# Cross attention: how the softmax sums are inverted, who multiplies, and where the first residual block is loaded

## The reference, cut to what matters

```
scores = q @ k.T / sqrt(32)          # 154 context rows, with a mask on the first 512 query rows of a batch
out    = softmax(scores) @ v         # = (exp(scores - max) @ v) / sum(exp(scores - max))
x2     = x1 + out @ Wo.T + bo        # projection and residual, done in the next stage
```

## Time and profile before

| | |
|---|---|
| time, median of 3 runs (lowest, highest) | 3250.19 us (3243.59, 3250.36) |
| the profiled execution: its time, its span | 3238.29 us, 3236.2 us |
| cross attention, first PE instruction to the next stage's first | 2386.25 to 2696.28 us |
| busy over the whole span: PE, DVE, ACT, POOL | 2957.8, 2091.0, 1609.1, 1750.3 us |
| busy in the 34 us from 2586 to 2620: PE, DVE, ACT, POOL | 33.55, 31.83, 25.63, 0.00 us |
| inversions L1525 in the whole stage | 64, 111.0 us busy |

### The profile page before, as it was taken

The page is one execution under the profiler, slowest core; times in us unless marked ns, Lnnn a source line. Parts: engine busy times, 40 slices in busy tenths (PEclk is TensorE's granted clock), DMA queues, the critical chain, the costliest instruction groups (busy, mean ns, idle before and its releaser), DMA issues. The chain is left out here.

```text
span 3236.2 us, 42137 instructions
## 1 busy us (share of the span) xinstructions
PE 2957.8 (91%) x15214; PEld 1738.2 (54%) x15214; DVE 2091.0 (65%) x3796; ACT 1609.1 (50%) x2996; POOL 1750.3 (54%) x742
## 2 busy tenths in 40 slices
PE   8999699999999999999999999969959997889388
PEld 5878355455455454554554555338745554777333
DVE  4332777777777777776777777436549894665323
ACT  2222166666667666666676666622227672222111
POOL 1000179788889797888897989830001102332265
PEclk9999599999999999999999999979969998999589
DMA  7444754745655647456456563438765442442621
GB/s 230 173 175 156 183 104 98 160 97 112 147 108 117 141 99 160 98 109 150 102 116 139 108 147 79 102 105 266 202 158 157 135 139 89 152 147 105 214 69 36
DMA packets 186936, 435.77 MB, mean 135 GB/s; under 512 B 30557, under 2 KB 51966, under 8 KB 166716
## 3 DMA queue, kind: packets, MB, share of 16 engines
q1 hardware_dynamic: 161718, 286.39, 30.6%
q0 software_dynamic: 24448, 145.80, 21.4%
q10 hardware_dynamic: 576, 1.05, 0.1%
HBM read 180.67 MB, written 127.18 MB: 95 GB/s over the span
## 5 line engine op out<-in xcount | busy, mean ns | idle before, releaser
L791 DVE TENSOR_REDUCE part_max<-ps_s 128x1 f32<-128x512 f32 x2048 | 1269.6, 682 | 351.8 <-PE ps_s L692 351.6
L891 ACT ACTIVATE probs<-ps_st 128x512 f32<-128x512 f32 x2048 | 1059.9, 602 | 542.5 <-PE ps_st L711 536.7
L641 POOL TENSOR_TENSOR added<-added,probs 128x2048 f32<-128x2048 f32 x256 | 1181.7, 4616 | 105.0 <-ACT probs L891 83.0
L711 PE MATMUL ps_st<-q_stack,k_stack 98*128 98x512 f32 x2048 | 873.8, 430 | 6.6 <-ACT probs L891 5.3
L692 PE MATMUL ps_s<-k_stack,q_stack 96*128 96x512 f32 x2048 | 832.3, 413 | 22.7 <-POOL max_parts L631 20.8
L711 PEld LDWEIGHTS ps_st<-q_stack,k_stack 98*128 98x128 f32 x2048 | 391.7, 192 | 526.0 <-ACT probs L891 357.4
L722 PE MATMUL ps_pv<-probs,v_sb 128*32 128x512 f32 x4096 | 551.6, 611 | 0.0
L692 PEld LDWEIGHTS ps_s<-k_stack,q_stack 96*128 96x128 f32 x2048 | 400.0, 195 | 120.7 <-DVE part_max L791 35.6
L649 POOL DMA_DIRECT2D probs<-probs x128 | 111.3, 874 | 193.3 <-PE ps_pv L722 175.6
L722 PEld LDWEIGHTS ps_pv<-probs,v_sb 128*32 128x32 f32 x4096 | 81.0, 108 | 163.9 <-ACT probs L891 135.7
L641 POOL TENSOR_TENSOR added<-probs 128x2048 f32<-128x2048 f32 x32 | 146.6, 4580 | 23.9 <-ACT probs L891 23.9
(11 more groups left out here) (274 smaller groups left out, 3512.2 us busy)
## 6 DMA issues: line engine op xcount, KB each, us to landing
probs<-probs POOLq DMA_DIRECT2D x128, 1024.0 KB, 7.1
xq_stack<-q_parts SPq DMA_DIRECT2D x64, 384.0 KB, 4.7
q_parts<-k_stack SPq DMA_DIRECT2D x88, 256.0 KB, 4.1
q_stack<-q_hi SPq DMA_DIRECT2D x64, 256.0 KB, 6.6
k_stack<-k_hi SPq DMA_DIRECT2D x64, 256.0 KB, 9.4
x_in<-in_x_rows SPq DMA_DIRECT2D x8, 1024.0 KB, 7.2
q_hi<-qk_h_out SPq DMA_DIRECT2D x8, 1024.0 KB
q_lo<-qk_l_out SPq DMA_DIRECT2D x8, 1024.0 KB, 6.3
```

The source lines that it names most:

```text
L641: pool.tensor_tensor(added[:, w % 2], left, probs[:, k % RING], ALU.add).then_inc(added_up, 1)
L711: pe.matmul(ps_st[:, n % BANKS], k_stack[0:TOP, w // BPB, j, k * P:(k + 1) * P], q_stack[:, w % 4, j], start=True, stop=True).then_inc(ite ...
L791: dve.tensor_reduce(part_max[:, s:s + 1], ps_s[:, (w * SLOTS + s) % BANKS], AX.X, ALU.max)\
L891: act.activation(probs[:, k % RING, j], ps_st[:, n % BANKS], ACT.Exp, scale=SCALE).then_inc(item_used, 1)
```

## The change

Units are now treated in pairs p (units 2p and 2p+1), for the first 15 pairs:

- The two units' sums, one row per head, go by DMA to DRAM (`sums_to_columns`) and come back as a 128x32 tile `dens_c` (`columns_back`). DVE inverts that tile once a pair (`invert(p)`). The inverses go out again (`inverses_out`) and are read back into `attn_out`, each head's row spread on its 32 partitions by one of four DMAs (`inverses_spread`). POOL multiplies `attn_out` with the weighted values, 128x1024 at once, and SP stores the two units.
- The weighted values wait in six buffers instead of two. `sums_out` waits for the DMA of the sums instead of the multiplication.
- The last two units are inverted and multiplied by DVE, each inversion as one instruction of 128x512, after the split of the preloaded block and only when the stores of all 15 pairs have landed.
- POOL's weight splits stand behind the products of pairs 1, 3, 4, 6 and 7.
- The first block of x1 is no longer loaded in cross attention. `shared_feed_forward` loads it, 1 MB, as its very first DMA, ahead of the six small loads.

```diff
-        for u in range(UNITS + 3):
+        def sums_to_columns(p):
+            sp.wait_ge(sums_done, 2 * p + 2)
+            sp.dma_start(dens_rows, sums[0:P:HD]).then_inc(dens_moved, 16)
+        def columns_back(p):
+            sp.wait_ge(dens_moved, 16 * (p + 1))
+            sp.dma_start(dens_c[:], dens_rows.rearrange("j w (c e) -> (j w c) e", e=PER)).then_inc(dens_laid, 16)
+        def inverses_out(p):
+            sp.wait_ge(inverted, p + 1)
+            sp.dma_start(recip_rows.rearrange("j w (c e) -> (j w c) e", e=PER), dens_c[:]).then_inc(recip_moved, 16)
+        def inverses_spread(p):
+            if p:
+                sp.wait_ge(out_stored, 32 * p)
+            sp.wait_ge(recip_moved, 16 * (p + 1))
+            for j in range(HEADS):
+                sp.dma_start(attn_out[j * HD:(j + 1) * HD], recip_rows[j].partition_broadcast(HD)).then_inc(recip_loaded, 16)
...
+        for u in range(UNITS):
+            if u % 2 and u >= 3:
+                sums_to_columns((u - 3) // 2)
+            if u % 2 == 0 and u >= 4:
+                inverses_out((u - 4) // 2)
             if exists(u + 1):
                 rows_into_place(u + 1)
+            if u % 2 and u >= 3:
+                columns_back((u - 3) // 2)
+            if u % 2 == 0 and u >= 4:
+                inverses_spread((u - 4) // 2)
+            if u % 2 and u >= 5:
+                store((u - 5) // 2)
...
-                        sp.dma_start(next_x[:, c], x1_rows.rearrange("(n t p) d -> n t p d", t=TPB, p=P)[0, c])\
-                          .then_inc(next_loaded, 16)
...
+        p = PAIRS - 2
+        inverses_out(p)
+        inverses_spread(p)
+        store(p)
+        store(p + 1)
...
+                for p in range(PAIRS - 1):
+                    pool.wait_ge(recip_loaded, 16 * HEADS * (p + 1))
+                    pool.wait_ge(raw_done, 2 * p + 2)
+                    r = 2 * p % RAWS
+                    pool.tensor_tensor(attn_out[:], attn_out[:], attn_raw[:, r:r + 2], ALU.mult).then_inc(normalized, 1)
+                    if p in SPLIT_AFTER:
+                        split(SPLIT_AFTER.index(p))
...
+                def normalize_last(u):
+                    w = u % 2
                     dve.wait_ge(sums_done, u + 1)
-                    dve.reciprocal(sums[:, u % 2, cols], sums[:, u % 2, cols]).then_inc(inverted, 1)
+                    dve.reciprocal(sums[:, w], sums[:, w]).then_inc(last_inverted, 1)
                     dve.wait_ge(raw_done, u + 1)
+                    dve.wait_ge(out_stored, 32 * (PAIRS - 1))
...
+                for u in range(UNITS):
                     for s in range(SLOTS):
+                        if s == 0 and u % 2 == 0 and u >= 4:
+                            invert((u - 4) // 2)
                         if exists(u + 2):
                             slot_max(u + 2, s)
...
-                    if u >= 2:
-                        act.wait_ge(normalized, u - 1)
+                    if u >= RAWS:
+                        act.wait_ge(normalized, (u - RAWS) // 2 + 1)
                     act.wait_ge(pv_done, u + 1)
-                    act.activation(attn_raw[:, u % 2], ps_pv[:], ACT.Copy).then_inc(raw_done, 1)
+                    act.activation(attn_raw[:, u % RAWS], ps_pv[:], ACT.Copy).then_inc(raw_done, 1)
...
+                sp.dma_start(x_in[:, 0], x1_blocks[0]).then_inc(first_loaded, 16)
                 for dst, src in ((ident[:], eye), (bias_raw[:, 0:D], b12.unsqueeze(0)), (bias_raw[:, D:2 * D], b3.unsqueeze(0)),
```

More of the change, by code:

```diff
@@ L1294, in cross_attention @@
         inverted, normalized = sem("xinverted"), sem("xnormalized")
[L1295 removed]
+        dens_moved, dens_laid, recip_moved, recip_loaded = (
+            sem(n) for n in ("xdens_moved", "xdens_laid", "xrecip_moved", "xrecip_loaded"))
+        last_inverted, last_normalized = sem("xlast_inverted"), sem("xlast_normalized")
+        out_stored = sem("xout_stored")
         def exists(u):
@@ L1398, in _, with split @@
                 pool.memset(ks_stack[ROWS:TOP + 1].bitcast(F32), 0.0).then_inc(ones_set, 1)
-                for n, (_, high, low) in enumerate(PARTS):
+                def split(n):
+                    _, high, low = PARTS[n]
                     pool.wait_ge(ahead_loaded[n % 2], 16 * (n // 2 + 1))
@@ L1558, in _ @@
                         max_rows(u + 2)
-                    if exists(u - 2):
-                        invert(u - 2, 1)
-                        normalize(u - 2)
+                invert(PAIRS - 2)
+                dve.wait_ge(next_high, 1)
+                dve.tensor_tensor(next_l, ahead_raw[:].rearrange("p a c d -> p (a c) d"), next_h.bitcast(F32), ALU.subtract)\
+                   .then_inc(next_low, 1)
+                for u in range(UNITS - 2, UNITS):
+                    normalize_last(u)
             @block.scalar
@@ L1744, in add_bias @@
                 def add_bias(i, u):
-                    if not first(i, u):
+                    if first(i, u):
+                        pool.wait_ge(first_loaded, 16)
+                    else:
                         pool.wait_ge(loaded[u], i * (16 * LOADS) + 16 * LOADS * u)
-                    rows = first_x if first(i, u) else x_in[:, u]
+                    rows = x_in[:, u]
                     for t in range(TPB):
```

65 lines of the change are left out of this document (30 added, 35 removed).

## The result

The changed kernel took 3291.69 us in the median of 6 executions (3252.32 to 3357.6), beside 3248.35 us for the kernel before (3240.27 to 3256.46). The ratio is 1.009, with a 95% interval of 1.0049 to 1.0132. The ratio leaves out executions more than 1.5% above the fastest of their kernel, here two of the six, so the medians lie further apart (1.3%) than the ratio says. The profiled execution took 3300.42 us, 62 more than that of before (3238.29).

The account below looks back on a forecast made before the run. The prediction took a loop of PE and ACT to bound cross attention, with DVE nearly full beside it. Its terms, -0.7 + 1.8 + 2.4 = +3.5 us, gave a median of 3253.7 us, about 3254, with 8 in 10 from 3242 to 3268.

Parts of the forecast that it names:

- The trip by way of DRAM: Cross attention's pairs: sums out, inverses back and POOL's product lie beside the loop, 0 us unless rows of maxima are late.
- The sum: Whole kernel: plain units, end and feed-forward start add up as -0.7 + 1.8 + 2.4 = +3.5 us.
- Rival B: Cross attention: rows of maxima land late behind spreads and query loads; +15, with the rest +18, 3269 us; chance 0.16.
- Plain units: Cross attention's 8.26 us units: DVE isn't in the loop, so relieving it buys only two waits, -0.7 us.
- Rival A: Cross attention's plain units: DVE does set the pace; -15 us, with the rest -12, about 3238 us; chance 0.13.
- The end: End of cross attention: the trip is on the path, since DVE waits for pair 14's stores; +1.8 us.
- The start of the feed-forward: Next stage's head: small loads that DVE and POOL await land later behind x1's 1 MB load; +2.4 us.
- Rival D: Cross attention: POOL's product holds up DVE's `max_rows`; +12 us, with the rest +15.5, 3266 us; chance 0.06.

Follow-up runs that it names:

- Experiment 5: Changed kernel with the query loads of units 4 to 31 issued by POOL's queue instead of SyncE's: 3316.65 us, ratio 1.0234 to the kernel before.
- Experiment 12: Changed kernel with the trip spread over one unit more, last product written over the sums, x1's block behind the small loads: 3246.66 us, ratio 1.0009.
- experiment 8: Kernel before with rows of maxima made late by awaited 128 KB loads, one at unit 7, two at unit 24: 3288.19 us, ratio 1.0136.
- experiment 9: Changed kernel run again unaltered: 3279.4 us, ratio 1.0076 to the kernel before; its profiled execution, the fastest, took 3243.93 us.
- experiment 1: Kernel before with DVE's inversions left out for the first 30 units: 3246.19 us, ratio 1.0007.
- experiment 10: Kernel before with only x1's first block loaded at the head of the feed-forward, ahead of its small loads: 3247.85 us, ratio 1.0011.
- experiment 7: Changed kernel with each unit's sums sent out by their own DMA once copied: 3292.8 us, ratio 1.0092 to the kernel before.
- experiment 11: Changed kernel with the last two units' product written over the sums and x1's first block loaded behind the small loads: 3311.0 us, ratio 1.0091.

## Why the prediction was wrong

The forecast was 3254 us with a range up to 3268; the time was 3291.69. The step that failed is *The trip by way of DRAM*: "All of this lies beside the loop: 0, as long as the rows of maxima aren't held up". It went wrong in three places.

- **The length of a hop.** I took out and back as 4.39 us from self attention's last trip, whose queue had nothing else to do. In the changed kernel the way out alone takes 6.4 us at 2651.30, behind 1.5 MB in one queue. Experiment 5 shows that it isn't the queue alone: with the queries on POOL's, a way out took 7.7 us. My sentence that the columns are there at 2606.7, with 2.9 us of slack before the next rows, held in the quiet stretch (columns inverted by 2587.5, next rows at 2590.50), where units last 8.26 us. The four stops lie where keys, weights or `attn_t` are loaded besides, though not each such load brought one: that at 2594.79 (weights) and those at 2621.69 and 2631.55 (`attn_t`) did not. The trace of before had the sign of it: unit 6's rows landed 3.4 us after their last issue.
- **SyncE's own waits.** The sum had no term for them. SyncE takes its queue in order, so while it stands in one landing, rows, sums and queries behind it aren't issued. From 2400 to 2740 it stood 36.8 us in 16 landings of the two hops, and at 2651.89 this made the rows 1.4 us late at their issue. Experiment 12, with the same bytes and later demands, had no such stop.
- **The price of a stop.** Rival B had the late rows, over 3.4 us after their last issue, and put them down to the bytes ahead of them. Here they landed 4.1 us after it; that bytes alone don't do it is experiment 12. B was given 0.16 and +18 us, because I priced a stop at its own length. Stops for rows were 0.80, 0.86, 0.85 and 1.95 us in the profiled execution, 4.5 in all and under B's 15. The two long pieces, which hold the stops of 0.85 and 1.95, grew by 62.7 us together, nearly 60 of it the clock behind them. Experiments 8 and 9 show the two apart: a stop and some 42 us behind it, and three stops with nothing behind them.

The other steps by themselves:

- *Plain units*, "DVE isn't in the loop": right. The unit is 8.26 us, and experiment 1 gives 1.0007. Rival A was rightly refused, but its price was mis-added: 16.0 us of waits in 90 us are 1.5 us a unit, 35 us in 24 units and not 15.
- *The end*, +1.8: the mechanism was right, the size short. In the profiled execution it was 10.33 - 8.28 = +2.05, but there the low clock had made DVE's own start late. At the full clock (experiment 9) DVE waited 4.00 us, and from its start at 2684.30 to 2696.43 it took 12.13, +3.85. There the spreads took 5.3 us from the first issue to the product (2680.79 to 2686.06), where the sum had 3.9, and the stores 3.2 us behind the product (2688.4 to 2691.65), where it had 2.8. With the product written over the sums DVE's part is 8.20, though the stage still ends 1.4 us later than before.
- *The start of the feed-forward*, +2.4: it measured +1.8 at the first CAST in the changed kernel and +1.4 in experiment 10. By `h_out`, which is what the following work waits for, it is +2.7 and +2.3: this term was right. Loading x1's block behind the small loads brings the CAST to 7.91 but leaves `h_out` at +1.3.
- Without a fall the changed kernel stands at +7.5 from unit 0 to `h_out` (experiment 9: 2.1, 3.75 and 1.7), where the sum had +3.5 and no stops.
- *Rival D* went the other way round. DVE wasn't held up by POOL's product, but the last product took 4.28 us instead of 2.37 beside DVE's two-input subtraction (2737.22, 2.29 us). The Trainium skill, "SBUF — State Buffer", section "SBUF: two separate sides", says that the later of the two blocks fully. The trace agrees: the product began 0.24 us behind the subtraction and lost 1.9 us, about the 2.05 that were left of it.

Open is what decides whether the clock falls after a given stop, and for how long. In the middle of the stage, stops of 0.80 and 0.86 us in the changed kernel, of 0.94 in experiment 7, 1.09 in experiment 11 and 1.32 in experiment 9 had no fall behind them; 0.85, 1.21, 1.32 (experiments 5 and 11), 1.37, 1.62, 1.95 and 3.03 had. The length of the stop alone doesn't decide it. The same kernel gives 3244 in one execution and 3349 in another.

## What to carry to other kernels

Price a transfer by the landing times of its own stretch and queue, not by an idle one, and let nobody ask for it before about the slowest of them: the same bytes and hops cost nothing that could be measured once each landing was asked for 5 to 7 us after its issue instead of 3. Price a possible stop of PE by the granted clock that may follow it, not by its length. And before moving work off an engine, leave that work out once: VectorE at 94% wasn't in the loop and had nothing to give.

## What the runs showed of the hardware beyond that

- One stop of 3.03 us on PE, between stretches at a clock of 1.00, was followed by the 1.2 GHz level for the remaining 110 us of the stage, although PE was 100% busy in 100 of them (2630 to 2730). At the beginning of the same stage, stops of 2.43 and 2.30 us were followed by 3 to 4 us of it.
- In each traced fall of the changed kernel the clock was 1.00 up to the end of the stop and 0.50 within 2 us behind it; in experiment 8 it fell within the 3.03 us of the stop.
- Moving transfers to another engine's queue didn't help. With the queries on POOL's queue a hop on SyncE's still took 7.7 us, and the kernel stood 2.3% above the one before; with the hops on POOL's queue, where the sums' way out took about 4 us (2455.88 to 2459.83) but was issued later, it stood 4.4% above. The changed kernel stood 0.9% above.
- The same hop of 16 KB landed 1.4 to 7.1 us after its issue within one execution (experiment 12, inverses out), and 3.6 to 7.6 us in the changed kernel.
